# A graph layer with 25 node quads on one core: the unit sizes of the dense edge half and the places of the quads in the edge loop are changed

## The reference

```python
neigh = segment_sum(layernorm(x)[src], dst)
h = (1 + eps) * layernorm(x) + neigh
h = relu(h @ W1 + b1) @ W2 + b2           # 256 -> 512 -> 256
x = x + batchnorm(h) * gamma + beta        # mean and variance over all nodes
x = x + moe_ffn(layernorm(x))              # top 1 of 8 experts, 256 -> 1024 -> 256, capacity 1.25 T / 8
```

## Time and profile before

| | |
|---|---|
| median of 3 runs | 2602.64 us (2600.25 to 2615.07) |
| the profiled execution | 2600.25 us, its span 2598.6 us |
| busy | PE 1705.6 us (66%), DVE 1466.8 (56%), ACT 688.5 (26%), POOL 1732.5 (67%) |
| POOL's gathers, line 735 | 1240, busy 1186.2 us |
| idle before them | 407.5 us, of which "issue" 363.8 |

### The profile page before, as it was taken

One profiled execution on the slowest core, in us unless ns is written; L12 is line 12 of the kernel. 1 busy time (PEld: TensorE's weight loads), 2 busy tenths in 40 slices (PEclk: granted clock), 3 DMA queues, 4 the chain that ended last, 5 costly groups with the idle time before them and its releaser, 6 DMA issues. The chain is left out here.

```text
span 2598.6 us, 32998 instructions
## 1 busy us (share of the span) xinstructions
PE 1705.6 (66%) x9167; PEld 1044.7 (40%) x9168; DVE 1466.8 (56%) x4306; ACT 688.5 (26%) x1087; POOL 1732.5 (67%) x1716
## 2 busy tenths in 40 slices
PE   0034545755666666667668768675664889989984
PEld 0022323333333333334334334344552566656663
DVE  7867642547226624542562332336883877768884
ACT  6620000100011001100101112115664455455542
POOL 1057777777777777777777776742554678677866
PEclk9988767876887788789879899886656999999997
DMA  7634457544754575456445533325763122321130
GB/s 233 216 102 120 121 161 230 182 121 138 227 193 122 153 235 183 121 179 201 142 154 186 171 102 96 104 59 174 221 200 114 35 71 78 100 82 58 62 97 13
DMA packets 202984, 361.17 MB, mean 139 GB/s; under 512 B 63573, under 2 KB 127403, under 8 KB 202790
## 3 DMA queue, kind: packets, MB, share of 16 engines
q0 software_dynamic: 70464, 185.02, 24.0%
q1 hardware_dynamic: 130182, 172.61, 20.5%
q10 hardware_dynamic: 2144, 1.05, 0.1%
HBM read 291.08 MB, written 75.58 MB: 141 GB/s over the span
## 5 line engine op out<-in xcount | busy, mean ns | idle before, releaser
L735 POOL DMA_INDIRECT e_got<-table,e_idx x1240 | 1186.2, 957 | 407.5 <-issue 363.8
L797 PE MATMUL e_sums<-e_got,e_hot 128*128 128x256 f16 x1920 | 363.6, 370 | 372.3 <-DMA e_got<-table,e_idx 317.2
L797 PEld LDWEIGHTS e_sums<-e_got,e_hot 128*128 128x128 f16 x1920 | 241.2, 130 | 500.9 <-DMA e_got<-table,e_idx 350.6
L974 DVE SCALAR_TENSOR_TENSOR nodes<-e_sums,above,nodes 128x256 f32 (+1 forms) x161 | 77.3, 480 | 607.4 <-PE e_sums L797 396.0
L1630 POOL TENSOR_TENSOR x_midl<-x_midf,x_midh 128x512 f16<-128x512 f32 x200 | 291.4, 1485 | 94.1 <-ACT x_midh L1749 90.0
L902 ACT ACTIVATE e_hT<-e_up 128x1024 f32<-128x1024 f32 (+1 forms) x25 | 25.2, 1006 | 1083.3 <-PE e_up L846 1083.3
L1038 DVE TENSOR_TENSOR counts<-counts,e_tally 128x490 f32 x220 | 159.3, 724 | 125.1 <-PE e_tally L825 114.3
L825 PE MATMUL e_tally<-w2f 128*128 128x490 f16 x328 | 107.2, 445 | 170.4 <-DVE w2f L1027 169.6
L1706 PE MATMUL x_down<-x_w2h,x_midh 128*128 128x256 f16 x736 | 203.7, 277 | 18.9 <-DVE x_yb L1849 12.2
L1706 PE MATMUL x_down<-x_w2h,x_midl 128*128 128x256 f16 x736 | 203.5, 277 | 0.0
L1706 PE MATMUL x_down<-x_w2l,x_midh 128*128 128x256 f16 x736 | 203.5, 277 | 0.0
(11 more groups left out here) (214 smaller groups left out, 2847.4 us busy)
## 6 DMA issues: line engine op xcount, KB each, us to landing
w1f<-table SPq DMA_DIRECT2D x120, 512.0 KB, 4.5
e_got<-table,e_idx POOLq DMA_INDIRECT x1240
slot_rows<-e_zero SPq DMA_DIRECT2D x64, 268.0 KB, 3.3
x_row<-slot_rows SPq DMA_DIRECT2D x32, 536.0 KB, 7.4
table<-n_pair SPq DMA_DIRECT2D x25, 512.0 KB, 3.0
counts<-in_x SPq DMA_DIRECT2D x24, 512.0 KB, 4.6
r_xin<-in_x SPq DMA_DIRECT2D x24, 512.0 KB, 5.1
out<-r_row SPq DMA_DIRECT2D x24, 512.0 KB, 3.2
```

Of the source, the lines that this page charges most:

```text
L735: pool.indirect_dma_start(got[:, r, t, :], None, table.rearrange("p h d -> (p h) d"), bass.IndirectOffsetOnAxis(ap=idx[:, r, t:t + 1], axi ...
L797: ins = nc.tensor.matmul(sums[:, place, 0:D], hot[:, place, t, :], got[:, r, t, half * D:(half + 1) * D], start=(t == 0 and half == 0), st ...
```

## The change

The number of counting iterations of units 1 to 4 goes from 5, 4, 4, 3 to 8, 6, 5, 4, with 8 tiles in each instead of 10 to 14; the number of tiles of each unit, 64, 48, 40 and 32, stays. With the four mixed iterations behind each unit, the last spread moves from iteration 43 to iteration 50. Every quad stands now at or behind its old place, nearly all at r = 2, and quads 0 and 1 go from iterations 43 and 46 to 50 and 51. `closed_before` now counts a quad as closed from the first group of its iteration on. VectorE no longer waits for its own last window sum (`s_add`) before it copies a quad.

```diff
-UNIT_TILES = ((24, 24, 24, 24, 16, 16, 16), (14, 14, 12, 12, 12), (12,) * 4, (10,) * 4, (11, 11, 10))
+UNIT_TILES = ((24, 24, 24, 24, 16, 16, 16), (8,) * 8, (8,) * 6, (8,) * 5, (8,) * 4)
...
-AT = {2: (9, 2), 3: (13, 1), 4: (16, 1), 5: (19, 1), 6: (21, 2), 7: (24, 0), 8: (26, 1), 9: (28, 2), 10: (30, 2),
-      11: (32, 2), 12: (34, 1), 13: (36, 0), 14: (38, 0), 15: (39, 2), 16: (41, 0), 17: (42, 2), 0: (43, 1),
-      18: (44, 1), 19: (45, 2), 1: (46, 1), 20: (47, 0), 21: (48, 1), 22: (49, 2), 23: (51, 0)}
+AT = {2: (10, 2), 3: (14, 2), 4: (17, 2), 5: (19, 2), 6: (22, 2), 7: (24, 2), 8: (27, 2), 9: (29, 2), 10: (31, 2),
+      11: (33, 2), 12: (35, 2), 13: (36, 2), 14: (38, 2), 15: (40, 2), 16: (41, 2), 17: (43, 2), 18: (45, 2),
+      19: (46, 2), 20: (48, 2), 21: (49, 2), 0: (50, 0), 22: (50, 2), 1: (51, 0), 23: (51, 2)}
...
-    return max([0] + [QN * (q + 1) for q, (it, r) in AT.items() if it * RG + r <= group])
+    return max([0] + [QN * (q + 1) for q, (it, _) in AT.items() if it <= group // RG])
...
-                def quad(q, turns):
+                def quad(q):
                     k = ORDER.index(q)
                     if k > 0:
                         measure(ORDER[k - 1])
-                    dve.wait_ge(s_add, turns)
                     nc.vector.tensor_scalar(hrow.rearrange("p t d -> p (t d)"), nodes[:, q, :], 1.0, None,
                                             ALU.mult).then_inc(s_hrow, 1)
```

More of the change, by code:

```diff
@@ L1097, in _ @@
                         for q in quads_at(n, r):
-                            quad(q, n * RG + r + 2 if n * RG < SINGLE else turn)
+                            quad(q)
                 dve.wait_ge(s_sum, turn)
@@ L1101, in _ @@
                 then(add_window(dve.snap(dve.snap(dve.snap(turn) + 1) % 2), group_no(dve.snap(last_group))))
-                quad(NQ - 1, turn)
+                quad(NQ - 1)
                 measure(NQ - 1, N - (NQ - 1) * QN)
```

## The result

The changed kernel takes 2673.4 us in the median (2666.6 to 2674.6, 4 runs), the kernel before beside it 2604.1 us (2600.3 to 2615.1, 4 runs): 1.0254 times, with an interval of 1.0219 to 1.0289. The forecast was 2656, with 2636 to 2674 as its range, so the median lies 0.6 us inside its upper end. In two later batches of runs the changed kernel was 1.0240 (1.0216 to 1.0264) and 1.0228 (1.0195 to 1.0261) times the kernel before; the medians there are 60 and 57 us apart, against 69 here.

The account below looks back on a forecast made before the run. POOL's gathers bound the stretch to 1723.9 us, the chain of quads the end. Quad 21's start at 1682.3 plus 133.4 us of tail put the barrier at 1815.7, 53.7 later: 2656 us, range 2636 to 2674.

Parts of the forecast that it names:

- The middle: POOL's waits during the gathers: 6 us gained, with bounds of 15.2 us gained and 5 us lost.
- The gaps: Between the tail's quads, 21 to 24: windows, sums, spread, statistics and copies take 7.5, 13.4, 5.3, 3.6 and 3.6 us.
- The quads: Tail up to the barrier: quads 21, 0, 22, 1 and 23 take 17.1 us each, 85.5 us.
- rival 4: In the tail, each of five quads begins at the lower clock level, 12 us more: 2668; 5%.
- The signs: Five full quads, gaps 4 to 13 us, last gather 10 to 20 us later, tail near 78, middle waits 5 to 15.
- Behind the barrier: The stages after the edge stage get the same work, so their 836.6 us stay.
- The counting: Tiles spread over 30 iterations instead of 23 free nothing but POOL's waits, at most 15.2 us.
- The removed wait: VectorE's wait ahead of 24 copies was long over: worth 0, at most 1.5 us less.
- Rivals 1: Gathers run free and the quads hide beside them, all 15.2 us of waits go: 2587, faster; 4%.
- rival 2: Only quads 1 and 23 lie behind the last gather, one quad and its gap more, 21 us: 2624; 7%.
- Rival 3: Quads at r = 2 hold POOL 2 to 3 us wherever they meet pieces, 20 us more: 2682; 10%.
- Rival 5: The plan is refused and the general loop does all edges in a second pass, over 1500 us more; below 1%.

Follow-up runs that it names:

- late_hot: Only quads 0 and 1 moved, from (43, 1) and (46, 1) to (50, 0) and (51, 0), against the kernel before: 1.0112 times its time.
- spaced_2: 18 quads moved apart so that none hold POOL, against the kernel before, with its unit sizes, wait and bound rule: 0.9961 times its time.
- changed_2: The changed kernel itself run once more in a later batch, nothing altered: 1.0240 times the kernel before.
- changed_3: The changed kernel itself run once more, beside the version with the wait put back: 1.0228 times the kernel before.
- with_wait_2: VectorE's wait for its own last sum put back ahead of the copies, against the changed kernel, in a later batch: 1.0253 times the kernel before.
- old_places_2: The changed unit sizes put into the kernel before, with only quads 0 and 1 moved, to (50, 0) and (51, 0): 1.0155 times the kernel before.
- old_units_2: Old unit sizes, with quads 0 and 1 at (44, 0) and (47, 1), against the changed kernel: 1.0179 times the kernel before.
- with_wait: VectorE's wait for its own last sum put back, against the changed kernel, in the first batch with late gathers: 1.0091 times the kernel before.

## Why the prediction was right, point by point

- **POOL sets the stretch of gathers, the quads the end.** Right. Moving two quads to the end (late_hot) made the barrier 36 us later and the time 30 us longer, and taking waits away (spaced_2) made the barrier 4.5 us earlier in the profile and the time 10 us shorter.
- **The middle.** 6 us gained by forecast. Of the waits ahead of group 153 there are 12.1 us left of 15.2, so 3 gained. The wait of 5.9 us went, as told. Of the two new ones at quads 15 and 16 (at 1454 and 1468) the first, 3.5 us, came the way that was told, from 34.8 us between the starts of the quads. The second, 4.2 us, did not: it is ScalarE's clearing behind quad 16, which the prediction had nowhere, and so are 5.5 us ahead of groups 72 and 73, behind quad 6. Here the size of the middle came close while part of its cause was missed. Group 146 starts at 1643.05, told 1640.3. Quad 21 starts at 1682.59, told 1682.3; two misses cancel, by luck: quad 20 starts 1.9 us late, and the three groups behind it with their pieces took 17.5 us and not 19.1. In changed_2 quad 21 starts 5 us later, in changed_3 2 us.
- **The gaps.** 33.4 us told, 34.3 measured. Most of the difference lies in the gap with the spread, 8.2 for 7.5; VectorE pauses 0.7 us ahead of the spread. In the gap between quads 0 and 22, 13.9 for 13.4, the last two windows took 2.4 and 3.6 us: the fast form, taken for every window from group 150 on, did not hold for them. The gap hardly shows it, since its model in the earlier trace rows had a window of 3.4 us in it too.
- **The quads.** 17.1 us each told, 85.5 in all; measured 90.9. This is the term that was too small. The first product took 9.34 us in quad 0 and 8.77 in quad 1 instead of 7.13, as rival 4 had it for all five quads (12 us); four came longer, by 2.7, 1.6, 0.8 and 0.3 us. So the crowded tail did not stay at the fast level, by which the prediction had let rival 4 fall away. The granted clock, third from the right in the table by stretch, was 0.83 over quad 0 and 1.00 over quad 23 (the full clock, 2.4 GHz; the other level, 1.2 GHz, is 0.50):

```profile
1708.70:1728.50 19.80, 17.91 (x41) 8.03 (x42) 4.11 (x20) 3.77 (x5) 4.71 (x5) 0.83 0.14 41
1787.20:1804.30 17.10, 15.21 (x40) 6.73 (x40) 0.62 (x2) 3.77 (x5) 0.00 (x0) 1.00 0.00 0
```

TensorE had stood idle for 4.5 us ahead of quad 0's turning, but only for 1.5 ahead of quad 1's, so what makes a quad begin slow stays open. It comes again: changed_2 and changed_3 have slow first products in quads 0 and 1, with_wait_2 in quads 21, 0 and 23, of 8.6 to 9.0 us.

- **The barrier** came 60.4 us later, told 53.7: 5.4 of the 6.7 us are slow quads, 0.9 gaps, 0.3 the start.
- **The signs** came: five full quads with gaps of 3.5 to 13.9 us, the last gather 19.3 us later, the tail 79.2 us for 78, 12.1 us of waits ahead of group 153. POOL's wait ahead of group 154 was 17.8 us and not 14.6, since quads 21 and 0 took 3.5 us more than told.
- **Behind the barrier** nothing was to change. The profile has 10.8 us more there, but two more profiles of the changed kernel have 840.3 and 840.5, and the nine at POOL's pace have 836.6 to 847.4, so it is no effect of the change that could be told from this spread. The profile that the sum started from had the shortest of all. The profiled execution came out 17.5 us above the sum's 2654: 6.7 before the barrier and 10.8 behind it. That the median still lies in the range, by 0.6 us, is luck. The 53.7 us by which the kernel was to be slower stand closer to the 60 and 57 of the later batches than to the 69 of the first comparison.
- **The counting** freed nothing by itself (old_places_2 is not faster than late_hot), but with it the quads at r = 2 cost less: with the old sizes (old_units_2) the last gather ends 29 us later than in the kernel before. "Free nothing but POOL's waits" missed that the sizes also decide which quad stands ahead of a clearing.
- **The removed wait** was worth 0, as told, as far as the profiles show. The new `closed_before` was not run by itself.
- **Rivals 1 and 2** are out by the tail of 79 us. For rival 2 the prediction counted seven windows with gaps of 2 to 3 us between quads 22 and 23; the earlier trace rows and the rest of that timeline have eight, with 0.4 to 2.8 us. Rival 3 is out by 12 us of waits in the middle. With the old unit sizes a loss of its size came (44 us), but most of it where counting begins behind a quad, and not where a quad meets pieces. Rival 4 came in part, for two quads of five. Rival 5 is out, since a second pass of over 1500 us would show.

## What to carry to other kernels

Work that hides beside a paced stream of transfers is free only as long as the stream lasts. Before moving it later, count what then lies in the last few steps: here each of the two quads moved there by themselves cost 15 to 18 us, where a quad takes 17. And do not judge two parts of a schedule apart from each other: the late places cost 44 us of waits with the old unit sizes and 12 with the new ones. Look also at what stands behind the moved work in the program of an engine that is not busy: ScalarE's 7 us of clearing behind a quad kept VectorE waiting for over 20 us and, through it, TensorE and POOL.

## What the runs showed of the hardware

The same programs ran in two regimes. In the first batch the kernel before took 3155.9 us (29 runs, 3133 to 3190) instead of 2610. It is not a matter of the chip alone: the last batch ran at POOL's pace on the chip of the first. POOL's waits in with_wait, whose program is that of with_wait_2:

```profile
POOL e_got L735 <- PE e_sums L797: 205.0, 17, 25.9
POOL e_got L735 <- PEq L819: 147.0, 18, 17.8
POOL e_got L735 <- remote: 120.1, 34, 5.1
POOL e_got L735 <- DMA e_idx<-rows_of: 85.7, 14, 8.7
```

The gathers themselves were issued as fast as ever, busy 1184.5 us, but these waits sum to 533 us beyond the issue time of 0.3 us each; the stages behind the barrier took 854 to 858 us, only 2% more. "Remote" stands where the semaphore was raised by nothing that the trace records; no profile at POOL's pace has it, and here it may be a transfer whose record is missing. What made the gathers land late was not tried and stays open. The changed kernel with the wait put back cost 0.9% in this regime instead of 2.5%, and for spacing the quads no gain is shown (0.9962 to 1.0034).
